# Recurrence, dense mixture and last norm of a chained kernel joined in one stage, with the mixture's down products in full fp32

## The reference, cut to what matters

```python
def _L3_attn_ref(resid, norm_w, skip_w, in_w, conv_w, ...):      # recurrence
    x = resid * lax.rsqrt(jnp.mean(resid * resid, -1, keepdims=True) + EPS) * norm_w
    skip = x @ skip_w.T
    xc = causal_conv4(x @ in_w.T) + conv_b                        # 256 channels
    xs = jax.nn.silu(xc)
    delta = jax.nn.softplus(xs @ wd1.T @ wd2.T + wd2_b)
    Bm, Cm = xs @ wb.T, xs @ wc.T                                 # 16 states each
    # for each step l: h = exp(d_l * A) * h + (d_l * x_l) * b_l ; y_l = sum_n h * c_l
    y = (y + xs * W_D) * jax.nn.silu(skip)
    return resid + y @ out_w.T

def _L3_ffn_ref(x, Wr, br, W1, b1, W2, b2):                       # dense mixture
    probs = jax.nn.softmax(x @ Wr + br, axis=-1)                  # 8 experts
    gate = probs * keep                                           # top-p 0.8
    h = jax.nn.relu(jnp.einsum('bth,ehf->betf', x, W1) + b1)      # 512 hidden each
    y = jnp.einsum('betf,efh->beth', h, W2) + b2
    return jnp.einsum('bte,beth->bth', gate, y)

x = _layernorm(x + _L3_attn_ref(x, ...))
x = _layernorm(x + _L3_ffn_ref(x, ...))
```

## Time and profile before

| | us |
|---|---|
| median of three runs | 2514.3 (2511.88 to 2516.66) |
| span of the profiled execution | 2563.1 |
| first scan of stage 7 starts | 1607.48 |
| last step of stage 7 on VectorE starts | 2139.95 |
| first hidden tile of stage 8 on VectorE starts | 2156.19 |
| last step of stage 8 on VectorE starts | 2543.75 |
| last step of norm 8 on VectorE starts | 2559.74 |

### The profile page before, as it was taken

How to read it: one execution, slowest core, us unless ns; L and a number is a source line. 1 busy time by engine, 2 the same in 40 slices (tenths; PEclk the granted TensorE clock), 3 DMA queues, 4 the chain that set the end, 5 groups by cost and what they waited for, 6 DMA issues and landing times. The chain is left out here.

```text
span 2563.1 us, 34519 instructions
## 1 busy us (share of the span) xinstructions
PE 2219.2 (87%) x11662; PEld 1634.9 (64%) x11662; DVE 1785.8 (70%) x3554; ACT 1356.2 (53%) x2900; POOL 972.0 (38%) x795
## 2 busy tenths in 40 slices
PE   7887778899899999999994984798989887999998
PEld 3564657687798888888883772333333334777776
DVE  6667556677566676666654772788888896877776
ACT  6231223698444454445433442566666654878787
POOL 4000000221222323332322451898989984222222
PEclk9798899899899999999985996899999998999999
DMA  9400000000000000000001233332232330011112
GB/s 346 148 1 1 1 1 1 1 1 1 19 1 1 10 2 10 10 11 1 11 10 36 70 132 91 93 83 81 84 87 84 85 84 10 23 46 48 44 49 59
DMA packets 63335, 120.17 MB, mean 47 GB/s; under 512 B 7896, under 2 KB 29544, under 8 KB 62120
## 3 DMA queue, kind: packets, MB, share of 16 engines
q1 hardware_dynamic: 58776, 108.50, 14.3%
q0 software_dynamic: 4384, 9.46, 1.1%
HBM read 105.74 MB, written 31.65 MB: 54 GB/s over the span
## 5 line engine op out<-in xcount | busy, mean ns | idle before, releaser
L234 POOL TENSOR_TENSOR TMP<-TMP 128x512 f32<-128x512 f32 (+2 forms) x496 | 639.7, 1313 | 639.4 <-ACT TMP L225 457.9
L210 PE MATMUL ps<-TMPr 128*128 128x512 f32 (+4 forms) x2672 | 680.2, 404 | 77.0 <-DVE TMP L230 27.2
L210 PEld LDWEIGHTS ps<-TMPr 128*128 128x128 f32 (+2 forms) x2672 | 500.8, 192 | 257.9 <-issue 64.3
L210 PE MATMUL ps<-TMP 128*128 128x65 f32 (+5 forms) x4354 | 518.5, 287 | 14.2 <-DVE TMP L233 7.8
L210 PEld LDWEIGHTS ps<-TMP 128*128 128x128 f32 (+3 forms) x4354 | 476.5, 192 | 67.2 <-issue 32.5
L225 ACT ACTIVATE TMP<-ps,W 128x256 f32<-128x256 f32 (+2 forms) x528 | 284.2, 583 | 286.1 <-DVE TMP L230 156.0
L210 PE MATMUL ps<-TMP,W 128*128 128x512 f32 (+5 forms) x720 | 367.0, 632 | 47.8 <-POOL TMP L234 12.1
L225 ACT ACTIVATE TMPr<-ps,W 128x512 fp32r<-128x512 f32 x352 | 242.7, 690 | 92.2 <-PE ps L210 72.7
L210 PEld LDWEIGHTS ps<-TMP,W 128*128 128x128 f32 (+3 forms) x720 | 123.3, 190 | 217.4 <-issue 156.0
L233 DVE SCALAR_TENSOR_TENSOR TMPr<-ps,SM,XK 128x512 fp32r<-128x512 f32 x256 | 190.2, 750 | 92.1 <-ACT XK L225 89.8
L210 PE MATMUL ps<-Wr 128*128 128x512 f32 (+1 forms) x768 | 197.9, 375 | 24.9 <-ACT TMP L225 14.9
(11 more groups left out here) (235 smaller groups left out, 2829.6 us busy)
## 6 DMA issues: line engine op xcount, KB each, us to landing
TMP<-rows SPq DMA_DIRECT2D x168, 256.0 KB, 3.5
sorted<-pad SPq DMA_DIRECT2D x8, 2304.0 KB
TMP<-gates SPq DMA_DIRECT2D x56, 256.0 KB, 3.3
TMP<-sorted SPq DMA_DIRECT2D x72, 72.0 KB
W<-wp SPq DMA_DIRECT2D x1, 4124.0 KB
XK<-results SPq DMA_DIRECT2D x16, 256.0 KB, 3.6
W<-wp SPq DMA_DIRECT2D x1, 3072.0 KB, 26.6
W<-wp SPq DMA_DIRECT2D x1, 2136.5 KB, 19.7
```

Source lines behind the costliest of these rows:

```text
L210: return nc.tensor.matmul(out, lhsT, rhs, start=start, stop=stop, **k)
L234: gtt = lambda o, a, b, op: nc.gpsimd.tensor_tensor(o, a, b, op)
```

## The change

Stage 8, norm 8 by `layernorm` and the two fences between them are gone. One function, `scan_moe_stage`, carries all three; it is scheduled in half groups. From group 29 on, each half group carries one unit of the mixture beside its scan; the units run chunk by chunk (8 experts times 4 units for one chunk, then the next). 198 units stand beside scans, 58 come after the last scan.

- A unit's up product is still three fp32r products. The hidden tile is made by one VectorE instruction, `hg = max(up, -b1) * gate`, out of one PSUM bank; the rest of the relu's bias and the down bias come in as one product for each chunk (`bias_in`: an 8-row table times the gates). The down product is one full fp32 product, added into one PSUM bank `po` that holds the whole chunk's sum over all 32 units. `join` adds it to XT.
- ScalarE's two activations and GpSimd's adds of stage 8 are gone. Splitting the weights of all experts is done once (8 copies on ScalarE, 8 subtractions on GpSimd, beside groups 17 to 24).
- In the recurrence the row C comes by DMA for all groups now (`Cr`, four buffers in SBUF), and TensorE's spreading product is gone; in the 11 of 16 groups that VectorE reads, it multiplies `Cr` (SBUF) by `Hb` (SBUF). The decay has two PSUM banks in place of three, and the next decay stands behind the scan that frees its bank.
- Preparation, norms, `out`, routing share one PSUM bank (`misc`, bank 7). Norms copy their centred chunk out first. Routing is done chunk by chunk. Gate rows are stored to memory and fetched back with a broadcast for every expert of every chunk (64 DMAs, 56 before).

```diff
-        Bb, Ub, Hb, Cb = ([ar(512) for _ in range(n)] for n in (4, 6, 4, 4))
-        Cr = [ar(512) for _ in range(2)]
-        pC, pn, Ab, Yp, pr = PS[1], PS[2], (PS[0], PS[3], PS[4]), PS[5:7], PS[7]
...
+        Bb, Cr, Ub, Hb, Cb = (more(n) for n in (4, 4, 6, 4, 6))
...
+        Ab, ups, po, Yp, misc = (PS[0], PS[3]), (PS[1], PS[4]), PS[2], PS[5:7], PS[7]
...
+        first_unit = 16 + 13
...
+        for g in range(-2, GN + 16):
+            u = 2 * (g - first_unit)
+            if u == 0:
+                plan += ahead(0)
             if g + 2 < GN:
                 plan.append(("head", g + 2))
...
+            for s in range(2):
+                if 0 <= g < GN:
+                    plan.append(("scan", (g, s)))
+                if 0 <= g + 1 < GN:
+                    plan.append(("decay", (g + 1, s)))
+                if s and 0 <= g < GN:
+                    plan.append(("read", (g, 0)))
+                if u >= 0:
+                    plan += behind(u + s)
+                if 0 <= g - 2 < GN:
+                    plan.append(("tail", (g - 2, s)))
+                    if (g - 2) % 16 == 15:
+                        plan.append(("output", ((g - 2) // 16, s)))
+                if u >= 0:
+                    plan += ahead(u + s + 1)
+                plan += beside.pop((g, s), [])
+                if s and 0 <= g < GN:
+                    plan.append(("read", (g, 1)))
+                if u >= 0:
+                    plan += down(u + s - 1)
...
+                elif step == "up":
...
+                    if n >= 2:
+                        e.wait_ge(*hid_dve.at(units[n - 2]))
...
+                    mm3(ups[n % 2], (W1h[:, o], W1l[:, o]), xparts[i % 2]).then_inc(*up_pe(a))
...
+                elif step == "down":
+                    i, x, c = a
+                    e.wait_ge(*hid_dve.at(a))
+                    mm(po, tile(W2, 4 * x + c), hg[nth[a] % 4], False, x == 7 and c == 3).then_inc(*dn_pe(a))
...
+                elif step == "decay":
+                    g, x = a
+                    i, n = divmod(g, 16)
+                    carry(e, g - 1, x)
+                    e.wait_ge(*dl_dve.at(i))
+                    if g:
+                        e.wait_ge(*h_dve.at((g - 1, x)))
+                    act(Ab[x], ch(sets[i % 2][2], x), ACT.Exp, scale=negA[:, x * 16 + n:x * 16 + n + 1]).then_inc(*a_act(a))
...
-                        tt(Cb[q % 4], pC, Hb[q % 4], ALU.mult).then_inc(*hc_dve((a, x)))
...
+                    tt(Cb[q % 6], Cr[g % 4], Hb[q % 4], ALU.mult).then_inc(*hc_dve(a))
...
+                elif step == "hid":
+                    i, x, c = a
...
+                    stt(hg[n % 4], ups[n % 2], nB1[:, unit:unit + 1], gd[q % 3], ALU.max, ALU.mult).then_inc(*hid_dve(a))
+                elif step == "join":
+                    x = ch(XT, a)
+                    e.wait_ge(*dn_pe.at((a, 7, 3)))
+                    e.wait_ge(*x_low.at(a))
+                    tt(x, po, x, ALU.add).then_inc(*join_dve(a))
```

More of the change, by code:

```diff
@@ L43 @@
 SPLIT = 4
-LAST = 8
+LAST = 7
 NTL = 72
@@ L2011, in stage5 @@
         return dict(pe=pe, dve=dve, act=scalar, pool=pool, sync=sync)
[L2016 to L2021, removed]
@@ L2730, in scan_stage, with put @@
         norm = lambda n, i: [(s, (n, i)) for s in NORM[n]]
-        NORM_AT = {6: (10, 12, 13, 14, 15, 15, 15, 16), 7: (3, 4, 5, 6, 7, 8, 9, 9)}
-        turning = {i: ((i + 1) % NCH, (i + 2) % NCH) for i in range(NCH)}
-        turning[6], turning[7] = (7, 2), (5, 3)
+        units = [(i, x, c) for i in range(NCH) for x in range(8) for c in range(4)]
+        NU = len(units)
+        nth = {a: j for j, a in enumerate(units)}
+        first_unit = 16 + 13
+        beside = {}
+        def put(g, half, *steps):
+            beside.setdefault((g, half), []).extend(steps)
@@ new lines, in scan_moe_stage, with ahead, behind @@
+        put(9, 0, ("bias_negated", 0))
+        for p in range(4):
+            put(10 + p, 1, ("bias", p))
+        put(14, 1, ("bias_sum", 0), ("bias_turn", 0), ("bias_rows", 0))
+        for x in range(8):
+            put(17 + x, 1, ("weights", x))
+        def ahead(j):
+            if j >= NU:
+                return []
+            i, x, c = units[j]
+            return ([("fetch", 8 * i + 2)] if i and x == c == 0 else []) + [("up", units[j])]
+        def behind(j):
+            i, x, c = units[j]
+            return [("hid", units[j])] + ([("fetch", 8 * i + x + 3)] if c == 3 and x < 5 else [])
@@ L2758, in scan_stage, with down @@
+        def down(j):
+            if j < 0:
+                return []
+            i, x, c = units[j]
+            out = [("bias_in", i)] if x == c == 0 else []
+            return out + [("down", units[j])] + ([("join", i)] if x == 7 and c == 3 else [])
+        for g in range(-2, GN + 16):
+            u = 2 * (g - first_unit)
+            if u == 0:
+                plan += ahead(0)
             if g + 2 < GN:
                 plan.append(("head", g + 2))
-            if 0 <= g + 1 < GN:
-                plan.append(("decay", g + 1))
@@ L2775, in scan_stage @@
+        for j in range(2 * (GN + 16 - first_unit), NU):
+            plan += behind(j) + ahead(j + 1) + down(j - 1)
+        plan += down(NU - 1) + norm(8, NCH - 1)
+        assert not beside, beside
         oe = of(plan, "open")
-        const = Sig(sem("s7_constants"), ("bias", "select", "A", "diagonals"))
+        const = Sig(sem("s7_constants"), ("bias", "A", "diagonals"))
         s_aexp = Sig(sem("s7_decay_exp"), ("A",))
@@ L2855, in pe @@
                     i = a[1]
+                    bank_free(e, step, a)
                     e.wait_ge(*n_xa.at(a))
```

926 lines of the change are left out of this document (358 added, 568 removed).

## The result

The changed kernel takes 2510.9 us (median of 17 runs, 2501.9 to 2521.5), the kernel before 2516.7 (17 runs, 2510.8 to 2522.3). The ratio is 0.9975, 95% interval 0.9963 to 0.9987: 6 us faster, where 52 were forecast (2462 us, range 2415 to 2530). The time lies in the range; of the expected gain only a ninth came.

A forecast was written before the change was run, and what follows sets the result against it. Stage 7 was taken as bound by GpSimd and its neighbours, stage 8 by TensorE; 1607.5 + 143 + 751 + 10 = 2511.5 us profiled, 52 less than before, so 2462 us, range 2415 to 2530.

The forecast's parts named there:

- The profiled span and the median: Whole kernel: the profiled execution is 48.8 us longer than the unprofiled median; that difference is carried over whole.
- The share: From the first unit on: TensorE is busy 95% of the time, so 713 us of work take 751.
- The waits: At each chunk's end: TensorE waits for VectorE some 1 us, eight times, counted within the 5% idle.
- TensorE is held at many turns: Rival, beside units: chores waiting for ScalarE and VectorE leave TensorE at 90%, 792 us, total 2504; chance 19%.
- The clock: Beside units: TensorE's granted clock at 1.0 where it was 0.96.
- TensorE's work: From the first unit on: TensorE's queue of products and transposes sums to 713 us.
- VectorE beside the units: Beside units: VectorE needs 5.8 us a group with longer reads, hidden under TensorE's 6.3.
- The reads: VectorE's reads with both inputs in SBUF: 0 to 0.57 us more each; beside units 0.35, 0.5 us a group.
- Groups 0 to 28: Groups without units: 124 us before, 0 to 38 more from reads and weight subtractions; 19 taken, so 143.
- Decay, gaps, end, queues: Fewer decay banks and DMA queues cost 0, gaps of 16.2 and 16.0 us go, last chunk's chain costs 10.
- The slower rival: Beside units: VectorE becomes the bound through port and decay, 7.4 us a group, total 2563; chance 15%.
- What would show it: Profile signs: first up product after 130 to 160 us, 6.3 to 6.7 us a group, TensorE idle 3 to 7%.

The follow-up runs named there:

- best: Changed kernel with TensorE's C rows in the first 29 groups, spread routing, GpSimd reading the tenth group, later row and last norm's product; 0.9816 of the kernel before.
- row_late: Changed kernel with the turning of the routing weights one group later and the next gate fetches half a group after that; 2501.7 us, 0.9940 of the kernel before.
- c_pe_first: Changed kernel with the C row made by TensorE in PSUM in the 29 groups ahead of the first unit; 19.5 us below the kernel before, ratio 0.9930.
- best_2: `best` with the weights' splits in every second group and chunk 0's hand-over one group later; 46.7 us below the kernel before, ratio 0.9813.

## Why the prediction was wrong

*The profiled span and the median.* Right, for a half-seen reason. The 48.8 us between the profiled execution and the median lay ahead of the change, so carrying the difference over whole was allowed. The failing steps are terms of the sum: 904 us forecast from the first scan (143, 751, 10), 949.5 measured (155, 785, 9). That the time lies in the range is luck: the range's upper part stood for a mild case of VectorE as the bound, which did not happen.

*The share: the step that failed most.* "I take 95%", 751 us, with a granted clock of 1.0. Measured: 785 up to the last product, so 713 is 0.91 of it. The 34 us over 751 are 10 of idle time (48 us against the forecast's 38) and 24 of busy time (737 against 713), most of that by the clock (below).

*The waits.* The mechanism is the rival "TensorE is held at many turns", but at one turn a chunk. "The steps of a chain stand half a group or more apart" overlooked that `route` part 2, `row` and `row_out` stand in one half group; I had 1 us a chunk for a bank there, not the 4.3. Of TensorE's 56 idle us in U 25 are at the row and 18 at up products. U falls by 17 us with the late row, by 9 more with the routing spread, by 13 more in `best` (the tenth group's reads, the last norm's product): 39 together, where 33 were missing. The single steps of 9 and 13 are not far above the 5 us between two traces of one kernel; the sum is.

*The clock.* I expected 1.0 beside units; it was 0.97. After the dry spell at the row TensorE ran at the lower level for a while (3.62 us for 1.88). From the granted clock of windows of 4 us I estimate that low passes made 17 us of the busy time in the changed kernel, 6 in `row_late` and 5 in `best`; TensorE's whole busy time went down by 7 and 11. So the row's waits of 25 us cost, beside their own time, 7 to 11 us of busy time.

*TensorE's work: nearly right.* 713 us. Less that estimate, busy time is 721 us in the changed kernel, 725 in `row_late` and 722 in `best` and in the kernel without reads and with the late row: 1 to 2% above the sum, whatever the plan.

*VectorE beside the units: right in sum, wrong as a cover.* I had 5.8 us a group against 6.3. Measured it is busy for 5.7 (90.7 of the 112 us from 1936 to 2048, so 0.81, at 7.07 a group), and the mean never held TensorE. With two banks for up products one unit is in stock, and a half group has 3.1 us by the forecast. A scan, a hidden tile and a read take 2.6 of them; the three pieces of routing shown above take 2.3, 2.2 and 1.3 more, which does not fit. I put the routing into a mean of 12 us a chunk; it stands in three half groups. Whether more units in stock would have covered it was not tried.

*The reads.* The bounds, 0 to 0.57 us more, hold for the means in the changed kernel: 1.17 us in the first groups (median 0.98) and 0.88 beside units (1824 to 2048 us; median 0.68), where GpSimd is busy half of the time, against 0.68 out of PSUM. Single reads reach 1.8, and the mean of 1.28 in the kernel before with DMA rows is just above them. Beside units I took 0.35, and the mean is longer by 0.20. The Trainium skill's rule ("SBUF — State Buffer", "SBUF: two separate sides") is borne out both ways: GpSimd's products went from 1324 to 1484 ns too. I had applied it to the reads and left out the routing's small operations, which take three to five times their 0.19 us in the pieces shown.

*Groups 0 to 28.* 143 forecast, 155.4 measured, inside the range 124 to 162: 31 us were added where I had 19. `c_pe_first` shows 13 of them as the reads' price. The other 18 were not taken apart. VectorE waits 12 us there for the decay, 10 for ScalarE's other activations and 5 for GpSimd; which of chunk 0's chain, the eight splits and ScalarE's turns makes them stays open. (`best_2` is 12 us faster in A than `best`, but only 1.5 than `c_pe_first`: it undoes what `best` had added there, and says nothing of these 18.)

*Decay, gaps, end, queues:* right. Beside units there is one wait of 1.5 us for the decay, and the gaps between the stages are gone. GpSimd waits 180 us for rows, which held no scan: up to 2400 us VectorE waits for GpSimd only at norms, 18 us in all.

*The slower rival* (VectorE the bound, by port and decay) did not come, as half of VectorE's reads stay at 0.68 us or below beside a GpSimd that rests half of the time. *What would show it:* first up product at 155 (130 to 160), TensorE idle for 6% up to the last product (3 to 7), VectorE's idle time ended by TensorE: all as forecast. Reads within 0.66 to 1.8 (I had 1.26 as the top), 7.07 us a group (outside 6.3 to 6.7), clock 0.97, VectorE 0.81 of a chunk (below 85): the last three told the miss. The first scan did move from 1607, but it moves in the kernel before too.

With the row, the routing and the first reads mended (`best_2`), the region takes 903.0 us (A 141.0, U 762.0), the forecast's 904 (143, 761), and 713 is 0.95 of its 753 us up to the last product. It is another plan with other reads, so this shows that the share of 95% could be had, not that each term was right.

## What to carry to other kernels

A share of busy time taken from another stage is not a term of a sum: list, for the bound engine, each instruction that waits for work of another engine in the same slot, and hold each such slot's load against the slot's length, not the mean load against the mean. When a second engine is nearly as loaded as the bound one, a saved microsecond on the first is worth a part of it (here 110 us of products left out gave 76). And compare from the first instruction that the change touches, since what lies ahead can differ by more than the effect.

## What the hardware did that I had not expected

A small VectorE operation with both inputs in SBUF stood, in one place, for as long as GpSimd worked without a gap. In `best`, VectorE and then GpSimd (timelines):

```profile
1716.94 2.45 DVE L2893 TENSOR_TENSOR_SCAN TMP<-ps,SM,TMP 128x512 f32<-128x512 f32 x2
1719.30 7.07 DVE L229 TENSOR_TENSOR TMP<-TMP,W 128x32 f32<-128x32 f32 x1
1726.41 0.19 DVE L2795 TENSOR_REDUCE SM<-TMP 128x4 f32<-128x32 f32 x1
```

```profile
1720.17 1.27 POOL L233 TENSOR_TENSOR Wr<-W,Wr 128x512 fp32r<-128x512 f32 x1
1721.40 2.49 POOL L233 TENSOR_TENSOR TMP<-TMP,W 128x512 f32<-128x512 f32 x2
1723.84 1.26 POOL L233 TENSOR_TENSOR TMPr<-XT,TMPr 128x512 fp32r<-128x512 f32 x1
1725.06 1.26 POOL L233 TENSOR_TENSOR TMP<-TMP 128x512 f32<-128x512 f32 x1
1728.62 1.27 POOL L233 TENSOR_TENSOR Wr<-W,Wr 128x512 fp32r<-128x512 f32 x1 [2.29 <-ACT Wr L227]
```

A 32-column addition took 7.07 us and ended where GpSimd's run ended (1725.06 + 1.26); the scans before it, with one input in PSUM, passed at 1.23 us each beside the same run. In `best_2` the same addition fell into a gap of 0.9 us in GpSimd's work (at 1708.85 us) and took 0.18 us.

And the stages ahead of the recurrence, which the change hardly touches, took 34 to 45 us longer in some sets of runs than in others for the same kernel (first scan of the kernel before at 1607.5 against 1562.5, of the changed one at 1592.7 against 1558.6), and once so on the same chip. Which of them is slower, and why, wasn't followed up.
